# Causal attention of a two-layer decoder on one Trainium2 core: block transposes on VectorE, value products over 32 keys in tiles of the array

## What is computed

```python
def _attention(x, wq, wk, wv, wo):
    b, t, _ = x.shape
    q = (x @ wq).reshape(b, t, HQ, K)
    k = (x @ wk).reshape(b, t, HKV, K)
    v = (x @ wv).reshape(b, t, HKV, V)
    ...
    scores = jnp.where(mask, scores, -jnp.inf) / np.float32(np.sqrt(K))
    p = jax.nn.softmax(scores, axis=-1)
    out = jnp.einsum('bghtT,bThv->btghv', p, v).reshape(b, t, HQ * V)
    return out @ wo
```

## Time and profile before

| | |
|---|---|
| Median of 3 runs | 1656.57 us |
| Profiled execution, as a run | 1654.72 us |
| Its span in the profile | 1652.9 us |
| TensorE busy | 1418.1 us (86%) |
| VectorE busy | 960.3 us (58%) |
| ScalarE busy | 761.2 us (46%) |
| GpSimd busy | 239.5 us (14%) |
| Mean granted clock of TensorE | 0.932 |

### The profile page before, as it was taken

One profiled execution on the slowest core, in us unless ns is written; L12 is line 12 of the kernel. 1 busy time (PEld: TensorE's weight loads), 2 busy tenths in 40 slices (PEclk: granted clock), 3 DMA queues, 4 the chain that ended last, 5 costly groups with the idle time before them and its releaser, 6 DMA issues.

```text
span 1652.9 us, 43828 instructions
## 1 busy us (share of the span) xinstructions
PE 1418.1 (86%) x17669; PEld 874.9 (53%) x17681; DVE 960.3 (58%) x2519; ACT 761.2 (46%) x1950; POOL 239.5 (14%) x219
## 2 busy tenths in 40 slices
PE   5888888696499999999948899898989899889855
PEld 3343443483266676766633466346643565346645
DVE  4364644324477776777733776566764675477633
ACT  1313133251266665666624276327723474337634
POOL 3011210123030030110010200030001200030025
PEclk9989999798699999999988999999998999899968
DMA  9600000023230100100022000000000000000021
GB/s 330 231 17 1 18 2 6 19 59 96 78 141 4 25 20 10 36 4 16 4 69 55 1 2 1 5 14 1 2 5 14 1 2 1 1 13 2 2 87 53
DMA packets 57655, 59.72 MB, mean 36 GB/s; under 512 B 27869, under 2 KB 43104, under 8 KB 56304
## 3 DMA queue, kind: packets, MB, share of 16 engines
q1 hardware_dynamic: 54640, 51.63, 9.9%
q0 software_dynamic: 2528, 5.27, 1.0%
q10 hardware_dynamic: 288, 0.03, 0.0%
HBM read 33.22 MB, written 24.14 MB: 35 GB/s over the span
## 4 chain that ended last, share of the span: by engine, by line
PE 71%; DVE 15%; issue 4%; ACT 3%; DMA 2%; SPq 2%; POOL 2%; ACTq 0%; POOLq 0%; DVEq 0%
PE ps L1132 7%; PE ps L1520 6%; PE ps L1539 5%; PE ps L501 5%; PE ps L1553 4%; PE ps L1112 4%; PE ps L1122 4%; PE ps L1153 4%; DVE arena L588 4%; PE ps L259 4%; PE ps L1508 3%; PE ps L475 3%; PE ps L1167 2%; PE ps L1562 2%; PE ps L803 2%
## 5 line engine op out<-in xcount | busy, mean ns | idle before, releaser
L1265 DVE TENSOR_REDUCE nmax<-ps 128x1 f32<-128x512 f32 x256 | 166.6, 683 | 58.5 <-PE ps L1122 57.9
L1596 ACT ACTIVATE arena<-ps,arena 128x512 f32<-128x512 f32 (+3 forms) x256 | 135.4, 531 | 117.3 <-DVE arena L1656 111.0
L1656 DVE TENSOR_REDUCE arena<-ps 128x1 f32<-128x512 f32 (+3 forms) x256 | 124.2, 486 | 76.3 <-PE ps L1524 74.2
L1225 ACT ACTIVATE arena<-ps,nmax 128x512 f32<-128x512 f32 x172 | 119.0, 692 | 83.6 <-DVE nmax L1265 82.5
L1539 PE MATMUL ps<-sqc,arena 128*128 128x128 f32 x640 | 106.1, 287 | 20.1 <-DVE arena L1664 19.8
L588 DVE TENSOR_REDUCE arena<-ps 128x8 f32<-128x1232 f32 x64 | 89.2, 1437 | 38.2 <-PE ps L463 38.0
L1273 DVE COPY arena<-ps 128x512 f32<-128x512 f32 x128 | 87.9, 687 | 38.9 <-PE ps L1132 37.3
L259 PE MATMUL ps<-identb 128*128 128x512 bf16 x408 | 108.5, 425 | 1.4 <-DVE kcol L709 1.4
L1664 DVE TENSOR_SCALAR arena<-arena 128x512 f32<-128x512 f32 (+3 forms) x256 | 100.8, 394 | 9.1
L1520 PE MATMUL ps<-arena 64*128 64x384 f32 (+3 forms) x512 | 105.1, 489 | 0.0
L600 DVE RECIPROCAL arena<-ps 128x128 f32<-128x128 f32 x8 | 7.7, 958 | 162.0 <-PE ps L501 162.0
(11 more groups left out here) (355 smaller groups left out, 2721.8 us busy)
## 6 DMA issues: line engine op xcount, KB each, us to landing
xs_d<-onehot SPq DMA_DIRECT2D x4, 2560.0 KB, 24.1
cw<-in_cw SPq DMA_DIRECT2D x2, 2048.0 KB, 13.2
rv<-in_rv SPq DMA_DIRECT2D x2, 1536.0 KB, 19.7
late<-in_gw SPq DMA_DIRECT2D x3, 1024.0 KB, 10.7
arena<-gs_d SPq DMA_DIRECT2D x23, 129.0 KB, 2.1
onehot<-q_s SPq DMA_DIRECT2D x96, 8.0 KB
arena<-xs_d SPq DMA_DIRECT2D x23, 64.0 KB, 1.8
xs_d<-arena SPq DMA_DIRECT2D x23, 64.0 KB, 1.6
```

The source lines that it names most:

```text
L1225: nc.scalar.activation(PB[k % 6], ps[:, k % 5, :], ACT.Exp, bias=nmax[:, u:u + 1], accum_out=rsum[:, b % 2, u:u + 1]).then_inc(SD["exp"], 1)
L1265: nc.vector.tensor_reduce(nmax[:, k % NU:k % NU + 1], ps[:, k % 5, :], AX.X, ALU.max, negate=True)\
L1596: nc.scalar.activation(TF["p%d" % (n % 2)][:, h * S:h * S + wd], ps[:, FSB[n % 2][h], 0:wd], ACT.Exp, bias=TF["nmax"][:, k4:k4 + 1], accum ...
L1656: nc.vector.tensor_reduce(TF["nmax"][:, k4:k4 + 1], ps[:, FSB[n % 2][h], 0:wd], AX.X, ALU.max, negate=True)\
```

## The change

Four things change in stage F, and nothing outside it but buffers.

- The probabilities are no longer transposed by TensorE through PSUM. VectorE transposes each 32x32 block in place within its row of blocks (`flip`, L1673 of the changed kernel), from SBUF to SBUF. Partition group g (32 partitions) then holds, for every block of 32 keys, the keys on partitions and its own 32 queries on columns.
- `values` multiplies over 32 keys at a time. Each product takes one row group g (32 partitions) and one half h of the columns of the array (64), so that eight tiles of it are addressed; row group g accumulates in bank 4 + g. A key block of tile t serves the query tiles t to 3, 128 to 32 columns. It is now done once for a whole pair, after its four units. Every row group needs v of all 32-key blocks, so SyncE makes four copies of v from SBUF to SBUF, in 16 transfers of 32 partitions (`sp_F`).
- The scaling by the reciprocal moves to ScalarE (`norm`, SBUF to SBUF), with one reciprocal on VectorE for both heads (`invert`). The copy out of PSUM is gone. p has four buffers, one for each width.
- All projections by wo stand at the end of the run, in bank 1, since banks 4 to 7 now belong to the value products. `scores` of unit n + 2 wait for the exponentials of unit n.

```diff
-                                           "ptc", "pv", "ao", "wo")}
+                                           "rec", "vd", "pv", "ao", "wo")}
...
-        TF = dict(t0=cut(S), t1=cut(S), u0=cut(S), u1=cut(S), v=cut(NT * HKV * KD), kr0=cut(S), kr1=cut(S),
-                  nmax=cut(4), rsum=cut(4), rinv=cut(4), p0=cut(2 * S), p1=cut(2 * S),
-                  **{f"q{i}": cut(S) for i in range(HQ * KD // P)}, ao0=q_t[:, :], ao1=tmp[:, :])
-        PTF = [[TF[n + str(h)] for h in range(2)] for n in "tu"]
-        yn = arena[:, ARENA - S:ARENA].rearrange("p (i n) -> p i n", i=NT)
+        PTW = 3 * (S - P) + S
+        PTF = [[cut(PTW) for _ in range(2)] for _ in range(2)]
+        free = used[0]
+        used[0] = 0
+        TF = dict(t0=cut(S), t1=cut(S), u0=cut(S), u1=cut(S), v=cut(NT * HKV * KD))
+        used[0] = free
+        TF.update(kr0=onehot[:, :, :].rearrange("p i n -> p (i n)"), kr1=dec_row[:, :],
+                  nmax=cut(4), rsum=cut(4), rinv=cut(4), **{f"p{i}": cut(2 * (i + 1) * P) for i in range(NT)},
+                  **{f"q{i}": cut(S) for i in range(5)})
+        TFQ = lambda a, b: TF[f"q{a}"] if a < 5 else (own4, other4, x4)[a - 5][:, b * S:(b + 1) * S]
+        VW = HKV * KD
+        V4 = [cw[:, NTT * (2 * P + 2) + i * NT * VW:NTT * (2 * P + 2) + (i + 1) * NT * VW] for i in range(3)]
+        V4.append(rv[:, 3 * B * S:3 * B * S + NT * VW])
+        yn = amask[:, :, :].rearrange("p t n -> p (t n)").bitcast(F32).rearrange("p (i n) -> p i n", i=NT)
...
                     pe.wait_ge(SF["qm"], b * 2 * NTQ + 2 * (4 + n) + 2)
+                else:
+                    pe.wait_ge(SF["exp"], b * 2 * NUF + 2 * (n - 2) + 2)
                 if n % NT == 0:
                     pe.wait_ge(SF["qr"], b * NTQ + a + 1)
...
+            def values(a):
+
+                pe.wait_ge(SF["t"], b * 2 * NUF + 2 * NT * (a + 1))
+                if a == 0:
+                    pe.wait_ge(SF["vd"], 16 * 16 * (b + 1))
                     pe.wait_ge(SF["qm"], b * 2 * NTQ + 2 * NTQ)
-                elif n % NT == 0:
+                else:
                     pe.wait_ge(SF["ao"], b * NTQ + a)
-                for j in range(i + 1):
+                for k in range(4 * NT):
+                    t = k // 4
+                    v0 = t * VW + (2 * a) % HKV * KD
                     for h in range(2):
-                        v0 = j * HKV * KD + (2 * a + h) % HKV * KD
-                        ins = nc.tensor.matmul(ps[HALVES[h], 4, i * P:(i + 1) * P], TF["v"][:, v0:v0 + KD],
-                                               PTF[n % 2][h][:, j * P:(j + 1) * P], start=(j == 0), stop=(j == i),
-                                               skip_group_check=True)
-                        if j == i:
-                            ins.then_inc(SF["pv"], 1)
+                        for g in range(4):
+                            rows = slice(GR * g, GR * (g + 1))
+                            m = PTF[a % 2][h][rows, t * (S - P) + k * 32:t * (S - P) + k * 32 + 1]
+                            ins = nc.tensor.matmul(ps[HALVES[h], 4 + g, t * 32:P], V4[k % 4][rows, v0 + h * KD:v0 + (h + 1) * KD],
+                                                   bass.AP(m.tensor, m.offset, [list(m.ap[0]), [S - P, NT - t], [1, 32]]),
+                                                   start=(k == 0), stop=(k == 4 * NT - 1), skip_group_check=True,
+                                                   tile_position=(GR * g, KD * h))
+                            if k == 4 * NT - 1:
+                                ins.then_inc(SF["pv"], 1)
...
-                ins.then_inc(SF["wo"], 1)
+                if a == NTQ - 1:
+                    ins.then_inc(SF["wo"], 1)
...
             for n in range(NUF):
-                a, r = n // NT, n % NT
-                flip(n)
                 if n + 2 < NUF:
                     scores(n + 2)
-                if n >= 1:
-                    values(n - 1)
-                if r == 2 and a >= 1:
-                    project(a - 1)
-            values(NUF - 1)
+                if n % NT == 1 and n > NT:
+                    values(n // NT - 1)
+            pe.wait_ge(SF["exp"], (b + 1) * 2 * NUF - 2)
+            for a in range(NTQ - 1):
+                project(a)
+            values(NTQ - 1)
...
                 act.wait_ge(SF["max"], b * 2 * NUF + 2 * n + h + 1)
-                if n >= 2:
-                    act.wait_ge(SF["t"], b * 2 * NUF + 2 * (n - 2) + h + 1)
-                nc.scalar.activation(TF["p%d" % (n % 2)][:, h * S:h * S + wd], ps[:, FSB[n % 2][h], 0:wd], ACT.Exp,
+                if n >= NT:
+                    act.wait_ge(SF["t"], b * 2 * NUF + 2 * (n - NT) + h + 1)
+                nc.scalar.activation(TF["p%d" % i][:, h * wd:(h + 1) * wd], ps[:, FSB[n % 2][h], 0:wd], ACT.Exp,
                                      bias=TF["nmax"][:, k4:k4 + 1],
...
+            def norm(n, h):
+                i = unit(n)[1]
+                wd = (i + 1) * P
+                k4 = n % 2 * 2 + h
+                act.wait_ge(SF["rec"], b * NUF + n + 1)
+                p = TF["p%d" % i][:, h * wd:(h + 1) * wd]
+                nc.scalar.activation(p, p, ACT.Copy, scale=TF["rinv"][:, k4:k4 + 1]).then_inc(SF["nrm"], 1)
-                act.wait_ge(SF["pv"], b * 2 * NUF + (a + 1) * 2 * NT)
-                if a >= 2:
-                    act.wait_ge(SF["wo"], b * NTQ + a - 1)
-                nc.scalar.copy(TF["ao%d" % (a % 2)], ps[:, 4, :]).then_inc(SF["ao"], 1)
+                act.wait_ge(SF["pv"], (b * NTQ + a + 1) * 8)
+                nc.scalar.copy(TFQ(a, b).rearrange("p (i g j) -> p g i j", i=NT, g=4),
+                               ps[:, 4:8, 0:P].rearrange("p g (i j) -> p g i j", i=NT)).then_inc(SF["ao"], 1)
 
             exp(0, 0)
             exp(0, 1)
-            exp(1, 0)
             for n in range(NUF):
                 if n + 1 < NUF:
+                    exp(n + 1, 0)
                     exp(n + 1, 1)
-                copy(n, 0)
-                copy(n, 1)
-                if n % NT == 0 and n:
+                norm(n, 0)
+                norm(n, 1)
+                if n % NT == 2 and n > NT:
                     gather(n // NT - 1)
-                if n + 2 < NUF:
-                    exp(n + 2, 0)
             gather(NTQ - 1)
...
+            def invert(n):
+                k4 = slice(n % 2 * 2, n % 2 * 2 + 2)
+                dve.wait_ge(SF["exp"], b * 2 * NUF + 2 * n + 2)
+                nc.vector.reciprocal(TF["rinv"][:, k4], TF["rsum"][:, k4]).then_inc(SF["rec"], 1)
+
+            def flip(n, h):
+                a, i = unit(n)
+                wd = (i + 1) * P
+                dve.wait_ge(SF["nrm"], b * 2 * NUF + 2 * n + h + 1)
+                if n == 0:
+                    dve.wait_ge(SF["qr"], b * NTQ + NTQ)
+                    dve.wait_ge(SF["vd"], 16 * 16 * (b + 1))
+                if a >= 2:
+                    dve.wait_ge(SF["pv"], (b * NTQ + a - 1) * 8)
+                nc.vector.transpose(PTF[a % 2][h][:, i * (S - P):i * (S - P) + wd], TF["p%d" % i][:, h * wd:(h + 1) * wd])\
+                    .then_inc(SF["t"], 1)
...
             for n in range(NUF):
-                if n + 1 < NUF:
-                    norm(n + 1, 0)
+                if n:
+                    flip(n - 1, 0)
+                    flip(n - 1, 1)
                 if n + 2 < NUF:
                     top(n + 2, 0)
+                    top(n + 2, 1)
                 if n + 1 < NUF:
-                    norm(n + 1, 1)
-                if n + 2 < NUF:
-                    top(n + 2, 1)
-
-            dve.wait_ge(SF["wo"], b * NTQ + NTQ)
-            ch(nc.vector.tensor_tensor(xn[:, :, :], ps[:, 7, :].rearrange("p (i n) -> p i n", i=NT), xn[:, :, :], ALU.add))
+                    invert(n + 1)
+            flip(NUF - 1, 0)
+            flip(NUF - 1, 1)
...
+        def sp_F(sp, b):
+            sp.wait_ge(SF["v"], b + 1)
+            for g in range(4):
+                for k in range(4):
+                    sp.dma_start(V4[k][GR * g:GR * (g + 1), :], TF["v"][GR * k:GR * (k + 1), :]).then_inc(SF["vd"], 16)
...
-            for b in range(B - 1):
-                sp.wait_ge(XA["E"]["kv"], (B + b) * 2 + 2)
-                load_ctx(b + 1, 1)
+            for b in range(B):
+                if b + 1 < B:
+                    sp.wait_ge(XA["E"]["kv"], (B + b) * 2 + 2)
+                    load_ctx(b + 1, 1)
+                sp_F(sp, b)
```

56 lines of the change are left out of this document (13 added, 43 removed).

## The result

The changed kernel takes 1710.41 us (median of four runs, 1705.07 to 1721.73) against 1658.4 of the kernel before: the ratio is 1.0345, with an interval of 1.0306 to 1.0384. It is 3.4% slower. The forecast was 1621 us, and its range ended at 1655.

A forecast was written before the change was run, and what follows sets the result against it. TensorE was taken as the bound, busy 83.0 of 89 us in a run. After the change 14.1 us, six head pairs of 9.0 and a tail of 11.0 gave 79.1 against 87.6 a run, hence 1621 us, range 1592 to 1655.

The forecast's parts named there:

- the price of the value products: TensorE's block of 128 value matmuls, 256 instructions as issued, per head pair: 2.45 us, from rounds of eight tiles.
- the one drawn from the Trainium skill: Value products at 25 ns start to start: 6.4 us a head pair, kernel near 1717 us; chance 0.02.
- P: Time of one head pair (four units) in the loop of a stage F run: 8.4 us walked, 9.0 chosen.
- the tail: End of a run, from the end of unit 30's exponentials to the final addition: forecast 11.0 us.
- T6: End of unit 6's exponentials, counted from a run's first scores: forecast 14.1 us.
- The walk of waits: Chain of waits through one head pair of the loop, across TensorE, VectorE and ScalarE: 8.4 us without falls of the clock.
- a fall: TensorE's clock dropping to 0.50 after a thin stretch in the loop: up to 1.7 us each time.
- rival 3: VectorE's block transpose of 4-byte elements takes more than one pass: 1855 us at four; 0.10 with anything else over 1% slower.
- T5: End of unit 5's two exponentials, counted from a run's first scores: forecast 11.9 us.
- rival 2: Clock falls in nearly every head pair, or value products issue-bound at 14.4 ns (3.7 us): 1635 us; chance 0.15.
- both rivals together: Clock falls in every head pair and issue-bound value products coming together for a while: up to 1655 us.
- slower: Outcome of the whole kernel losing over 1%, by the block transpose or anything else: chance 0.10.

The follow-up runs named there:

- e4_both: The changed kernel with half the value matmuls (tiles of 64 partitions, other values computed) and filler matmuls ahead of two scores per head pair: 1613.4 us, ratio 0.9757.
- e2_half: The changed kernel with tiles of 64 partitions instead of 32, so half the value matmuls and weight loads over the same columns (other values computed): 1637.3 us, ratio 0.9891.
- e1: The changed kernel with each head pair's value products in three pieces behind different units' scores, and the gather later, same instructions: 1653.44 us, ratio 0.9999.
- e6: The changed kernel with value products in three pieces, and the tail's projections placed between pieces of value products: 1642.4 us, ratio 0.9942.
- e7: The changed kernel with value products in pieces, tail reordered, and four fillers ahead of the third and fourth units' scores: 1651.73 us, ratio 0.9987.
- e3: The changed kernel with 6 and 5 unread filler matmuls ahead of the first two scores of a head pair: 1716.07 us, ratio 1.0357.
- e5: The changed kernel with tiles of 64 partitions, each value matmul split in two, so 256 per head pair again (other values computed): 1714.34 us, ratio 1.0372.

## Why the prediction was wrong

**The step that failed** is the price of the value products: "eight tiles at 128, 96, 64 and 32 columns then need about 110, 83, 57 and (held by issue, as I choose) 55 ns a round, eight rounds of each: 2.45 us". I had priced the array, and asked for issue only as a spacing between two neighbours. In the trace the mean block takes 5.36 us. The columns were priced well: with half the instructions the same columns take 2.69 us in e4_both. Of the 2.7 us more, 1.6 are the stall and 0.6 that 512 records come more slowly even without it (3.3 us at the full clock for 2.67); the low clock inside the blocks is worth about 0.5 (33.1 us in 32 blocks, half of it lost). What was missing is a limit on the sum of instructions, which a spacing over 64 instructions, as in the earlier trace rows, can't show. The figure to doubt was the count itself: 512 records in one piece, where the kernel before has 40 value matmuls and their loads for a head pair, and those in four pieces.

The rival that came nearest was the one drawn from the Trainium skill ("TensorE: Matmul & The Clock Gate", Part 1: start to start never under about 25 ns). Its number, 1717, stands 7 us from the result, and I had given it 0.02. That it is so near is in part luck: P would have been 12.4 and was 11.46, and with a last block of 6.4 us the tail would have been 15 and was 19.4. The trace shows that the rule is near in effect and not right as it is put. Neighbours do start much closer than 25 ns: in the tail the row at 1039.46 has 47 matmuls, and the group behind it starts at 1040.18, so they lie 15 ns apart. Over a whole block of 256 the mean is 21 ns (19 in the twelve blocks with the full clock throughout), and the stalls, which come by the count of records and go in e2_half, make it in part a price by the number of instructions. My refutation, "the trace disagrees, at 14.4 ns", compared a short stretch with a long one.

**The sum, term by term** (per run): T6 14.6 for 14.1, 0.5 more; P 11.46 for 9.0, six times 2.46 or 14.8 more; the tail 19.4 for 11.0, 8.4 more. That is 23.7 us a run and 95 in all. With 6 us more outside the runs than the sum had left there, 1621 becomes 1722, which is the profiled run (1721.7).

**P.** From e4_both to e2_half the fillers go, and P rises by 0.9 (8.80 to 9.68): that is the clock. The prediction chose 0.6, with up to 1.7 for a fall; this mechanism and its size were right. From e2_half to the changed kernel P rises by another 1.8 (to 11.46): that is the number of instructions, of which the prediction had nothing; 1.5 of it are the stalls (36.7 us in the 24 pairs of the loops). The walk of waits itself, 8.4, was 0.3 to 0.4 short, with the fillers' own work in the measured figure.

**The tail.** Of the 8.4 us too little, 1.7 remain in e2_half (12.7 for 11.0): the values of pair 6 are still running when unit 30's exponentials end, and the walk had let the projections begin at once. The other 6.7 go with the number of instructions again, in two blocks; 3.7 of them are stalls, and the rest I haven't taken apart. Six times 1.8 and 6.7, times four runs, is 70 us, where the runs of e2_half's profile are 69 us shorter.

**Right**: the block transpose costs what a maximum costs (682 ns for 512 columns; the forecast said near 0.69), so rival 3 was not it. VectorE's 7.0 us for a pair fit with 56.7 us for a run of eight. The copies of v are hidden: SyncE issues 16 of them between 935.4 and 945.0, each lands after 2.3 us, and the first block transpose begins at 953.57. T5 came as walked (11.9 forecast, 12.05 or 12.5 measured). The scaled copy was sized too low, 0.72 us at width 4 for 0.58, with no consequence, because ScalarE is no bound: 68 of 102 us.

```profile
L1673 DVE STREAM_TRANSPOSE arena<-arena 128x512 f32<-128x512 f32 x64 | 41.2, 682 | 0.0
...
L1610 ACT ACTIVATE arena<-arena 128x512 f32<-128x512 f32 x64 | 42.7, 723 | 0.0
```

**The chances.** Value products bound by issue were in rival 2, but with 14.4 ns as its worst price, so that even both rivals together stopped at 1655. Priced at the 25 ns that the Trainium skill gives there ("TensorE: Matmul & The Clock Gate", Part 1), the same mechanism would have reached into "slower". The 0.10 for slower was laid on the block transpose, the one operation that the trace lacked. The failure was not in an unknown operation but in a known one, more than six times as many of it (256 matmuls for 40).

**Open**: why the span outside the four runs is 9 us longer in the changed kernel (1308.7; 1292 to 1300 in e1, e2, e4, e6 and e7, and 1305 to 1306 in e3 and e5). It goes with the slow blocks, but I didn't look for its place. Open too is how e1_spread's 57 us divide, and why the matmuls of e5_split come more slowly.

## What to carry to other kernels

When a change trades columns for instructions, as small tiles of the array do, price the block twice: by its columns, and by its count of matmuls and weight loads together, at some 10 ns a record for some 500 in a row (4.9 to 5.6 us for 512 here; where stalls followed each other 256 records apart in the changed kernel it was 14.6 and 15.7 ns). Take the dearer. A spacing read off a short group says nothing on a long one; look instead for a group as long as yours. If the count binds, the same instructions laid out between others with many columns cost far less: here three pieces for one gave back 57 us, all that the change had cost, with no instruction removed, though only 19 of them are stalls.

And a loss that shows up plainly, like the low clock, needn't be the one that binds: fillers were worth nothing before the supply was mended and 24 us after it, and cost 9 us where the products had been spread.

## What the runs showed of the hardware

TensorE's instructions arrive in packets of 16 KB, 256 records each. A piece of 512 records (256 small matmuls with 256 weight loads) takes 5.4 to 5.6 us in the mean and 4.9 to 5.4 at the full clock, though without its stall it would need 3.3 (4.1 in e5_split). The difference appears as one idle stretch of mostly 1 to 2 us marked "issue" at a place where nothing is waited for, and in the changed kernel every one of them ends 1.2 to 1.6 us after the end of a packet. With 256 records in a piece, one piece to a head pair of 8.7 to 9.8 us, it is all but gone (one of 0.5 us in the 64 blocks of e2_half and e4_both). A short piece alone isn't enough: with 512 records to a head pair, in pieces of 128 and 256, e6_tail still has 20 stalls, 20 us together. The Trainium skill ("Runtime: NRT & Kernel Launch", section on instruction fetch mechanics) describes the refill in blocks of 16 KiB, which the packets of the trace agree with, and holds that it is hidden; here it is not, with 52 us of stalls in the changed kernel.

The block transpose of VectorE takes 682 ns for 128 x 512 float32 values, and 302 ns for 128 x 128, as much as one pass over the elements. The Trainium skill ("Vector Engine (DVE) Microarchitecture Reference", section on the reshape front-end) says one element per cycle per lane, and the runs agree as far as they can show it: a maximum over 512 columns takes 685 ns.
